# A two-layer graph transformer on one core: the node features leave SBUF during edge attention, and the gather ring, the query slots and the linear branch's projection are reorganised

## What is computed

```python
for l in range(2):                                   # graph transformer
    q = ((x @ Wq[l].T + bq[l]) * 0.125).reshape(n, 8, 64)
    k, v = (x @ Wk[l].T).reshape(n, 8, 64), (x @ Wv[l].T).reshape(n, 8, 64)
    scores = einsum("ehd,ehd->eh", q[dst], k[src])   # 53125 edges, sorted by dst
    p = exp(scores - segment_max(scores)[dst])
    agg = segment_sum(p / segment_sum(p)[dst] * v[src])
    x = batchnorm(x + agg @ Wo[l].T + bo[l])
    x = batchnorm(x + relu(x @ W1[l].T + b1[l]) @ W2[l].T + b2[l])
# linear-attention branch, on the same normalised input
q, k = softmax(xWq + bq), softmax(xWk + bk)          # over each head's 64 features
ctx = einsum("htd,hte->hde", k, v)
out = einsum("htd,hde->hte", q, ctx) / (q * k.sum(t)).sum(-1) + q
out = out @ Wp.T + bp
```

## Time and profile before

| | us |
|---|---|
| median of 3 runs | 3078.48 (3066.44 to 3080.36) |
| the profiled execution | 3074.23 |
| its span on the core | 3072.9 |
| layer 0's edge attention, first product after the mixq load to last value product | 517 to 1293 |
| layer 1's edge attention, first query gather to last value product | 1737 to 2418 |

### The profile page before, as it was taken

One profiled execution on the slowest core, in us unless ns is written; L12 is line 12 of the kernel. 1 busy time (PEld: TensorE's weight loads), 2 busy tenths in 40 slices (PEclk: granted clock), 3 DMA queues, 4 the chain that ended last, 5 costly groups with the idle time before them and its releaser, 6 DMA issues.

```text
span 3072.9 us, 78344 instructions
## 1 busy us (share of the span) xinstructions
PE 2655.1 (86%) x32605; PEld 2145.7 (70%) x32605; DVE 1625.6 (53%) x3272; ACT 1320.7 (43%) x3690; POOL 1114.1 (36%) x1130
## 2 busy tenths in 40 slices
PE   5999997999999999758899688888888578599998
PEld 4877885777777777546488577777777455477777
DVE  5236785555555555556512355555555646656553
ACT  3324443555555554422232255555555322244432
POOL 0000002666666666400001277777777211222110
PEclk8999998999999999979899899999999889699998
DMA  5642003899899998741024499999999431123211
GB/s 201 225 176 107 32 28 141 300 324 328 312 332 321 320 327 299 230 122 40 21 96 154 171 328 341 351 353 349 349 352 346 138 110 61 38 86 97 69 59 59
DMA packets 231795, 621.75 MB, mean 202 GB/s; under 512 B 39008, under 2 KB 45792, under 8 KB 231427
## 3 DMA queue, kind: packets, MB, share of 16 engines
q0 software_dynamic: 137088, 466.78, 42.5%
q1 hardware_dynamic: 94339, 149.78, 14.6%
HBM read 538.80 MB, written 103.39 MB: 209 GB/s over the span
## 4 chain that ended last, share of the span: by engine, by line
PE 59%; DMA 14%; POOL 9%; DVE 8%; issue 7%; ACT 2%; SPq 0%; DVEq 0%; POOLq 0%; ACTq 0%
PE ps L1179 5%; PE ps L574 5%; PE ps L575 5%; PE ps L576 5%; POOL Y L1096 4%; DMA aggd<-stage,segs 4%; PE ps L1222 4%; PE ps L1209 4%; DMA Y<-KVd,srcE 3%; PE ps L774 3%; PE ps L942 2%; PE ps L944 2%; PE ps L943 2%; PE ps L1186 2%; PE ps L1872 2%
## 5 line engine op out<-in xcount | busy, mean ns | idle before, releaser
L1096 POOL DMA_INDIRECT Y<-KVd,srcE x449 | 430.1, 958 | 231.8 <-issue 117.2
L1370 ACT ACTIVATE stage<-ps,stage 128x128 f32<-128x128 f32 x832 | 294.8, 366 | 113.8 <-PE ps L1186 110.7
L1351 ACT ACTIVATE work<-ps 128x512 f32<-128x512 f32 x309 | 179.8, 597 | 296.7 <-PE ps L1179 296.1
L1096 POOL DMA_INDIRECT WA<-KVd,srcE x186 | 179.0, 962 | 352.3 <-PE ps L576 266.6
L1351 ACT ACTIVATE G<-ps 128x512 f32<-128x512 f32 x315 | 182.1, 597 | 233.8 <-PE ps L1179 233.2
L1277 DVE COPY G<-ps 128x512 f32<-128x512 f32 x208 | 143.9, 692 | 250.9 <-PE ps L1186 248.3
L1179 PE MATMUL ps<-ident,Y 128*128 128x128 f32 x1796 | 251.6, 280 | 26.5 <-DMA Y<-KVd,srcE 17.7
L574 PE MATMUL ps<-Wh,xs 128*128 128x512 f32 x600 | 239.0, 398 | 30.5 <-DVE xs L514 30.5
L1179 PEld LDWEIGHTS ps<-ident,Y 128*128 128x128 f32 x1796 | 199.1, 143 | 64.5 <-issue 40.2
L575 PE MATMUL ps<-Wl,xs 128*128 128x512 f32 x600 | 236.7, 394 | 0.0
L576 PE MATMUL ps<-Wh,xs 128*128 128x512 f32 x600 | 236.6, 394 | 0.0
(11 more groups left out here) (383 smaller groups left out, 6783.8 us busy)
## 6 DMA issues: line engine op xcount, KB each, us to landing
KVd<-stage SPq DMA_DIRECT2D x96, 256.0 KB, 2.0
aggd<-work SPq DMA_DIRECT2D x6, 2048.0 KB, 7.4
Qd<-stage SPq DMA_DIRECT2D x48, 256.0 KB, 2.0
G<-aggd SPq DMA_DIRECT2D x48, 256.0 KB, 2.6
Y<-KVd,srcE POOLq DMA_INDIRECT x449
Y<-in_x SPq DMA_DIRECT2D x4, 1536.0 KB, 15.0
G<-mixq SPq DMA_DIRECT2D x24, 256.0 KB
mixd<-rowsb SPq DMA_DIRECT2D x24, 256.0 KB
```

The costliest lines, as they stand in the source:

```text
L1096: pool.indirect_dma_start(out=kvs[a], out_offset=None, in_=KVd[l][:, :], in_offset=bass.IndirectOffsetOnAxis(ap=srcE[:, n:n + 1], axis=0)) ...
L1351: act.activation(kT[n % len(kT)], banks(l)[place_of(l, "k", n) % len(banks(l))][:, :], ACT.Copy).then_inc(out_a, 1)
L1370: last = act.activation(pT[g % len(pT)][:, P * i:P * (i + 1)], SC[g % 2][:, P * i:P * (i + 1)], ACT.Exp, bias=smin[:, t:t + 1], scale=-1.0 ...
```

## The change

**Room.** Before each edge attention SP writes `xT` to DRAM (`put_x`), and after the attention reads it back (`get_x`), 6.4 MB each way, in both layers. `put_x(0)` stands behind the branch weights, ahead of the second store of Q; `put_x(1)` ahead of the first store of Q in layer 1. `get_x` stands in the join, behind the loads of the split rows. POOL and DVE wait for the write (`x_away`); DVE waits for the return ahead of its first addition to `xT` (`x_back_in`).

**Ring.** The K|V ring has 28 buffers in both layers. Landings are counted on 14 semaphores (`KVF`), so `fetch(n)` from the 15th on waits that tile n - 14 has been transposed, beside the wait for the buffer. Query rows and aggregated rows have three buffers each.

**POOL's order.** `fetch_slots` runs ahead by 2 (layer 0) or 3 blocks (layer 1). The fetches of a round stand ahead of its `fetch_slots` and `scatter`.

**Side work.** `BD`'s columns and divisor columns are one product of 130 columns for each quarter (three into PS[0], one into PS[1]). `Wp` is cut into a high and a low half once, the transposed result too, and the projection is twelve f32r products in place of four float32 ones. DVE gets two reciprocals and two multiplications for one of each, and one subtraction more per tile.

```diff
-KVN = (20, 25)
+KVN = (28, 28)
+KVF = 14
+NB = 3
@@ fetch (POOL)
                 if n >= KV:
                     pool.wait_ge(agg, NQ * l + (n - KV) // 4 + 1)
+                if n >= KVF:
+                    is_turned(pool, l, "k", n - KVF)
@@ fetch_slots (POOL)
-                if j:
-                    is_turned(pool, l, "q", j - 1)
+                if j >= NB:
+                    is_turned(pool, l, "q", j - NB)
@@ POOL's loop
-            at = KV
+            at = KVF
             for g in range(NQ + AGG_AT + 2):
-                j = (g + 3) // 2
-                if g % 2 and j < NJ:
+                while at < ET and at < KVF + LOOK[l] + 4 * (g + 1):
+                    fetch(at)
+                    at += 1
+                j = g // 2 + ahead
+                if g % 2 == 0 and j < NJ:
                     fetch_slots(j)
                 x = (g - 2 - AGG_AT) // 2
                 if g % 2 == AGG_AT % 2 and 0 <= x < NJ:
                     scatter(x)
-                while at < ET and (at - KV) // 4 <= g - AGG_AT:
-                    fetch(at)
-                    at += 1
@@ empty_agg (DVE)
-                if j or l:
-                    dve.wait_ge(sct, 16 * (NJ * l + j))
-                dve.tensor_copy(stage[:, 0, :], AG[:, :]).then_inc(ev, 1)
+                if j >= NB or l:
+                    dve.wait_ge(sct[j % NB], 16 * (uses(NJ, NB, j % NB) * l + j // NB))
+                dve.tensor_copy(aggrow[j % NB], AG[:, :]).then_inc(ev, 1)
@@ head_sp
             if e == 2 * NT + 1:
                 branch_weights_sp()
+                sp.wait_ge(xt_made, NT)
+                put_x(0)
@@ layer 1's stores (SP)
+        def x_done(e):
+            if e == 2 * NT:
+                is_normal(sp, 1, NCK - 1)
+                put_x(1)
@@ out_pe
-                    for f in range(4):
-                        pe.matmul(PS[0][0:r, P * f:P * (f + 1)], qT[:, f, 0:r], BD[:, f, 0:P], start=(f == 0),
-                    for f in range(4):
-                        mm = pe.matmul(PS[1][0:r, 2 * f:2 * f + 2], qT[:, f, 0:r], BD[:, f, P:P + 2], start=(f == 0),
+                    for f in range(3):
+                        pe.matmul(PS[0][0:r, 130 * f:130 * (f + 1)], qT[:, f, 0:r], BD[:, f, :], start=(f == 0),
+                    pe.matmul(PS[1][0:r, 0:130], qT[:, 3, 0:r], BD[:, 3, :], start=True, stop=True,
...
-                    mm = pe.matmul(PS[1][0:r, :], oT[:, k - 10, 0:r], Wp[:, k - 10, :], start=(k == 10), stop=(k == 13))
+                    pe.matmul(PS[1][0:r, :], hi, WpH[:, i, :], start=(i == 0), stop=False)
+                    pe.matmul(PS[1][0:r, :], hi, WpL[:, i, :], start=False, stop=False)
+                    mm = pe.matmul(PS[1][0:r, :], lo, WpH[:, i, :], start=False, stop=(i == 3))
```

More of the change, by code:

```diff
@@ L175, in build @@
         mixd = dram("mixd", [N, D])
+        xTd = [dram(f"xTd{l}", [P, 4, N]) for l in range(2)]
         nfd = dram("nfd", [ET, P])
@@ L658, in edge_views @@
             spare = [WA[:, w, 2 * i:2 * i + 2, :].rearrange("p a b -> p (a b)") for w in range(3) for i in range(2)]
+            moved = [xflat[:, 1024 * i:1024 * (i + 1)] for i in range(10)]
             if l == 0:
-                kvs = spare[0:4] + [pair(G, i) for i in (0, 2)] + kvs + [mt[:, 512:1536], pair(rowsb, 2)]
+                kvs = spare[0:2] + [pair(G, i) for i in (0, 2)] + kvs + [mt[:, 512:1536], pair(rowsb, 2)] + moved
                 kT += [G[:, 12 + i, :] for i in range(3)]
@@ L693, in build @@
         smin = stage[:, 1, 0:ET]
-        qslot = stage[:, 3, :]
+        tail = [xflat[:, 10240 + 512 * i:10240 + 512 * (i + 1)] for i in range(4)]
+        qslots = [stage[:, 3, :], tail[0], tail[1]]
+        aggrow = [stage[:, 0, :], tail[2], tail[3]]
         hotT = [hotTs[:, i, :] for i in range(3)]
@@ L697, in build @@
         snB = mt[:, 0:ET]
-        kv_in = [sem(f"kv_in{i}") for i in range(max(KVN))]
-        q_in, sct, seg_idx = sem("q_in"), sem("sct"), sem("seg_idx")
+        kv_in = [sem(f"kv_in{i}") for i in range(KVF)]
+        q_in, sct = [sem(f"q_in{i}") for i in range(NB)], [sem(f"sct{i}") for i in range(NB)]
+        seg_idx = sem("seg_idx")
         hot, turned, out_a, out_d = sem("hot"), sem("turned"), sem("out_a"), sem("out_d")
@@ L818, in out_act @@
                         act.wait_ge(m_b, t)
-                    act.activation(oT[:, :, 0:r], k4(PS[1][:, :])[:, :, 0:r], ACT.Copy).then_inc(m_oe, 1)
+                    act.activation(oT[0][:, :, 0:r], k4(PS[1][:, :])[:, :, 0:r], ACT.Copy).then_inc(m_oe, 1)
+                if t == 0 and 2 <= k < 6:
+                    if k == 2:
+                        act.wait_ge(g_in, 16)
+                    act.activation(WpH[:, k - 2, :], Wp[:, k - 2, :], ACT.Copy).then_inc(w_hi, 1)
                 yield
@@ L858, in kv_before, with filled_for @@
         def kv_before(l, a):
-            return l * (uses(ET, KVN[0], a) if a < KVN[0] else 0)
+            return l * uses(ET, KVF, a)
+        def filled_for(e, l, j):
+            e.wait_ge(filled, (7 + min(j, 1), 9)[l])
         def is_turned(e, l, kind, n):
@@ L895, in clear_slots @@
         def clear_slots(l):
-            dve.memset(qslot, 0.0)
+            dve.memset(qslots[0], 0.0)
+            if l == 1:
+                x_away(dve, l)
+                for slots in qslots[1:]:
+                    dve.memset(slots, 0.0)
             for i in range(2):
@@ L1127, in attend_pool @@
                 begin(pool)
+            x_away(pool, l)
             for n in range(early, early + 4):
                 fetch(n)
+            filled_for(pool, l, 1)
             fetch_slots(1)
-            for n in range(early + 4, KV):
+            for n in range(early + 4, KVF):
                 fetch(n)
-            at = KV
+            ahead = 2 + l
+            if l == 1:
+                fetch_slots(2)
+            at = KVF
             for g in range(NQ + AGG_AT + 2):
-                j = (g + 3) // 2
-                if g % 2 and j < NJ:
+                while at < ET and at < KVF + LOOK[l] + 4 * (g + 1):
[3 more added lines that the diff above has]
+                if g % 2 == 0 and j < NJ:
                     fetch_slots(j)
@@ L1398, in edges_stored @@
         def edges_stored(e, l):
-            e.wait_ge(sct, 16 * NJ * (l + 1))
+            for i in range(NB):
+                e.wait_ge(sct[i], 16 * uses(NJ, NB, i) * (l + 1))
         crowd_done = sem("crowd_done")
@@ L2096, in build @@
         qkv_pe(1, xs1, Wh1, Wl1, idle)
-        qkv_sp(1, idle)
+        def x_done(e):
+            if e == 2 * NT:
+                is_normal(sp, 1, NCK - 1)
+                put_x(1)
+        qkv_sp(1, x_done)
         area.close()
@@ L2127, in build @@
         join_sp(1)
+        get_x(1)
         join_dve(1)
```

84 lines of the change are left out of this document (59 added, 25 removed).

## The result

| | before | after |
|---|---|---|
| median of the runs made together, us | 3077.36 (3066.44 to 3080.36) | 3039.38 (3031.19 to 3043.71) |
| ratio, 95% interval | | 0.9885 (0.9846 to 0.9923) |
| the profiled execution, its span | 3074.23, 3072.9 | 3043.71, 3042.3 |
| layer 0: first gather into Y to the end of attention | 801.1 | 751.3 |
| from there to layer 1's first query gather | 438.0 | 458.2 |

The forecast was 3034 us, in a range of 2998 to 3076. The four lower rows, with the first gather into Y 11 us later (497.96 before, 509.01 after), add up to the difference of the spans: +11 - 50 + 20 - 14 + 2 = -31 us. The marks are POOL's: the gather with which its loads resume behind the branch, the first query gather, and the one-element memset of `crowd` that follows each attention (1299.03 and 2424.31 before, 1260.31 and 2392.04 after).

A forecast was written before the change was run, and what follows sets the result against it. It took PE and the K|V ring to bound layer 0, transfers close, and POOL layer 1. From 3074.2: loop -58, layer 0 tail -3, layer 1 -8, memsets +1, writes +12 and +14, clock +2 gave 3034 us, range 2998 to 3076.

The forecast's parts named there:

- The loop of layer 0, -58: Layer 0's attention: a group falls from 7.46 to 6.90 us over 104 groups, -58 us.
- The end at 7.25 us: Layer 0's loop, weak end: full transfers keep back half of PE's gain and waits, 7.25 us a group, -22 us.
- rival B: Transfers give nothing more in layer 0: a group takes 7.25 us, kernel 3070 us; chance 0.18.
- Side work, 1.4 us a tile: Linear branch on PE: merged divisor products and f32r projection save 1.4 us a tile, 0.35 us a group.
- Extra wait on each fetch, 0: POOL's K|V fetches: a second semaphore wait costs 0, at most +12 us.
- Layer 1, -8: Layer 1's attention, three query and row buffers: two early POOL stalls and about 3 us of tail go, -8 us.
- The write in layer 0, +12: Layer 0's Q phase: stores of Q queue behind the write of x, PE stands, +12 us (+6 to +22).
- in layer 1, +14: Layer 1's Q phase: write of x shares transfers with early gathers, PE stands, +14 us (+5 to +20).
- The read back, 0: Join: x lands before its first addition, 0, at worst +4 us for both layers.
- A: PE is the bound and the writes hide: a group takes 6.76 us, kernel 3002 us; chance 0.14.
- C: Writes of x run at 193 GB/s, 33 us each, with a 7.25 us group: kernel 3106 us; chance 0.08.
- D: Depth not delivered: layer 0 keeps landing waits, or two waits cost POOL 12 us in layer 1; 3066 us; chance 0.08.

The follow-up runs named there:

- old order, 20 buffers, old side work: Changed kernel with rings of 20 and 25, POOL's earlier loop order, separate divisor products and float32 projection: 3094.23 us, ratio 1.0068.
- old order, 20 buffers, new side work: Changed kernel with rings of 20 and 25 and POOL's earlier loop order, all else kept: 3072.62 us, ratio 0.9992.
- 28 buffers, old side work: Changed kernel with its rings of 28 but separate divisor products and float32 projection as before: 3058.41 us, ratio 0.9944.
- fewer bytes: Changed kernel with the side work's own loads and stores cut to 64 of 512 columns: 3039.05 us, ratio 0.9897.
- PE lighter still: Changed kernel with four projection products in place of twelve, those with low halves left out: 3013.08 us, ratio 0.98.
- quarters: Changed kernel with layer 0's x write at the linear branch's head and layer 1's cut into four pieces among the Q-phase stores: 3010.56 us, ratio 0.9798.
- quarters, rows emptied behind K: The quarters kernel with DVE emptying a block's aggregated rows behind the next group's K eviction instead of ahead: 2986.58 us, ratio 0.9727.
- the write in the branch: Changed kernel with layer 0's write of x moved to the linear branch's head, behind all stores of Q: 3027.81 us, ratio 0.985.
- the four corners: Old or new side work, with 28 buffers or with 20 and 25 in old POOL order: 3058.41 and 3039.38; 3094.23 and 3072.62 us.

## Why the prediction was right, and where its steps were off

Layer 0 per group, in us, all worked out from the stretch and the waits of PE from 560 to 1200 us (640 us, over a fifth of POOL's instructions), with the length of layer 0's attention in each profile beside them:

| kernel | group | PE busy | waits for landings | waits for DVE's bank | layer 0's attention |
|---|---|---|---|---|---|
| before (7.46 and 6.95 over the 700 us of the earlier trace rows) | 7.42 | 6.94 | 0.31 | 0.08 | 801.1 |
| old order, 20 buffers, old side work | 7.46 | 6.92 | 0.35 | 0.06 | 808.5 |
| old order, 20 buffers, new side work | 7.24 | 6.60 | 0.42 | 0.07 | 782.6 |
| 28 buffers, old side work | 7.16 | 6.79 | 0 | 0.33 | 768.6 |
| after | 6.99 | 6.50 | 0 | 0.35 | 751.3 |
| fewer bytes | 6.93 | 6.48 | 0 | 0.37 | 744.7 |
| PE lighter still | 6.71 | 6.12 | 0 | 0.35 | 716.5 |
| quarters | 6.90 | 6.47 | 0 | 0.35 | 743.9 |
| quarters, rows emptied behind K | 6.81 | 6.56 | 0 | 0 | 728.3 |

After, the write in the branch and the quarters have the same loop in layer 0 and took 751.3, 750.6 and 743.9 us for it. So a difference of 7 us between two profiles, or of 0.1 us a group, shows nothing by itself.

- *The loop of layer 0, -58.* Measured -50 in the profiles, and 55 by the medians of the four corners (3094 to 3039). The mechanism of the ring was right: the landing waits went, and half of POOL's stand with them. The value 6.90 for a group was nearly right (6.98) for a wrong reason, by luck. I had capped the gain by the transfers, between 6.80 and 7.00, and two runs show no such cap: fewer bytes gave nothing, and with PE lighter a group took 6.71 us at 357 GB/s. What PE stood for instead, 0.35 us a group, is the bank that DVE empties late; taking that wait away gave back a part of it, 16 us by the profiles and 24 by the medians. It was in the trace of before, 6.9 us on the same pair of lines, and I hadn't asked what it would become when PE no longer waited elsewhere: the kernels whose PE stands 0.3 to 0.4 us a group for landings have under 0.1 of the other wait, those without landing waits 0.33 to 0.37. PE's busy time fell by 0.44 us a group where I had 0.35. The end at 7.25 us, which is also rival B's group, was worked out wrongly: half of 0.35 + 0.35 kept back leaves 7.11, not 7.25. The 3 us of layer 0's tail were not measured apart; they are within the -50.
- *Side work, 1.4 us a tile.* The four corners give 19 to 22 us for it, 0.18 to 0.21 us a group, where the full 0.35 would be 36. PE's busy time fell by 0.29 to 0.32 between the corners; the time didn't follow all the way.
- *Extra wait on each fetch, 0.* Right: 0.305 us of gap with two waits, as with one.
- *Layer 1, -8, and its row buffers called slack.* Measured -14. The two stalls near the start are gone, as said. The 3 us of the last query gather are not seen: with three query buffers but one row buffer the part behind the last K|V gather was no shorter than before (30.9 against 28.8 us), and with three row buffers it was 24.1. The step that failed is "that is slack": with one row buffer layer 1 is 10 us longer. POOL bounds the middle, but what is left to do when the gathers end is time too, and there DVE's wait for the scatter before is on the path.
- *The write in layer 0, +12, and in layer 1, +14.* The landing was put at 221.5, the eviction ran at 221.91; the first gather came 11 us later. In layer 1 the write landed 27.5 us after its issue, where the working had 28, and the eviction waited 18.18 us; the Q phase and the join took 20 us more together, where 14 for the write, 1 for the memsets and 1 of the clock's 2 make 16. The two experiments took out 12 and 17 us of them, which is the direct measure.
- *The read back, 0.* Right: issued at 1269.57, landed 26 us later, and the first addition to x, at 1326.7, was released by PE.
- *The sum.* -40 said, -31 in the profiled pair, -38 in the medians. It came out close because errors cancelled: the loop and its tail gave 11 us less than said, layer 1 gave 6 more. No rival came. B's 7.25 us a group was too high, and its cause, full transfers, wasn't there. A's room in the transfers was there, but its 6.76 had no new wait of PE in it. C's 33 us a write were 25.4 and 27.5. D's landing waits in layer 0 and its price of two waits on POOL weren't there. One of my signs was wrong: POOL's waits for the value product were to be mostly gone, and they were halved, while the loop did get faster.

## What to carry to other kernels

When a wait is taken away from the bounding engine, look at what its other suppliers were doing in that time: a wait of 7 us in the trace of before, on a row that one would pass over, became 34 us, and moving one copy behind another on DVE was worth 24 us of the run by the medians. An order and a buffer depth are one decision: eight fetches ahead of a query gather cost nothing with 28 buffers and 113 us with 20. A large write costs what is queued behind it, so it goes where nothing is, or in pieces that the eviction buffers cover.

## What the runs showed of the hardware

- 6.4 MB between 128 partitions and DRAM moved faster than the 387 GB/s that I took. The write in layer 0, and the second half of the read back, in stretches of the kernel after:

```profile
207.00:212.00 5.00, 5.00 (x19) 3.94 (x18) 0.00 (x0) 0.00 (x0) 0.00 (x0) 0.74 1.03 435
1281.00:1286.00 5.00, 0.94 (x8) 0.85 (x8) 3.86 (x9) 1.02 (x2) 0.00 (x0) 0.50 0.99 418
```

  These rates are above the 358 GB/s that the Trainium skill gives for transfers between HBM and SBUF (DMA: Bandwidth & Descriptors, Where 436 GB/s comes from), which I had cited. Another page of the Trainium skill (HBM Reference, Specifications) says that a core streaming alone reaches about 425, and the trace agrees with that one, with 435 and 418. No stretch shown here with gathers of 4 KB rows went above 357. The first part of the read back was slower, 266 GB/s from 1275 to 1281, with the split rows beside it.
- The write took 26.2 us in the branch too, where its own queue was empty: POOL's four early K|V gathers ran beside it (it was issued at 268.02, they from 267.89 on). There it held nobody up.
- The share of the DMA engines is a poor measure of room: with 4.5% fewer bytes it was 0.93 for 328 GB/s, after 0.95 for 341, and the time was the same.
- POOL's query gathers and scatters lasted 1159 and 1209 ns in layer 0 after, where they had been 1054 and were 1034 with the old side work and 28 buffers, 1052 and 1054 with the new side work and 20. It depends on neither alone, and on what it depends I don't know; POOL had the time.
